# Two-attention decoder layer: an order by batch halves for the last three head groups, angles on GpSimd, and maxima turned in fp16

## The reference

```python
x = x + attn(_layernorm(x), Wq_down, Wq_up, Wq_rope, Wkv_down, Wk_up, Wv_up, Wk_rope, Wo)   # 128 heads
x = x + xattn(_layernorm(x), ctx, ctx, positions, Wq, Wk, Wv, Wo)                           # 32 heads, 8 kv heads
x = x + ffn(_layernorm(x), gate_w, base_w, base_b, lora_A, lora_B)                          # 8 LoRA experts, top 2
# attn: q_c = (x Wq_down) Wq_up, k_c and v_c from x Wkv_down: 4 wide per head; q_r = x Wq_rope: 64 per head
#       k_r = x Wk_rope, one for all heads; scores = (q_c k_c + q_r k_r) / sqrt(68); softmax; v_c; Wo
# xattn: rotary angles position * 10000^(-2i/16) turn q and k (head width 16); softmax; Wo
```

## Time and profile before

| | us |
|---|---|
| median of 3 runs | 869.03 (868.4 to 870.11) |
| the profiled execution | 867.85 |
| its span | 865.9 |
| TensorE busy | 803.9 (93%) |
| VectorE busy | 647.9 (75%) |
| ScalarE busy | 568.5 (66%) |
| GpSimd busy | 582.8 (67%) |

### The profile page before, as it was taken

How to read it: one execution, slowest core, us unless ns; L and a number is a source line. 1 busy time by engine, 2 the same in 40 slices (tenths; PEclk the granted TensorE clock), 3 DMA queues, 4 the chain that set the end, 5 groups by cost and what they waited for, 6 DMA issues and landing times.

```text
span 865.9 us, 17867 instructions
## 1 busy us (share of the span) xinstructions
PE 803.9 (93%) x5624; PEld 395.2 (46%) x5624; DVE 647.9 (75%) x1209; ACT 568.5 (66%) x1045; POOL 582.8 (67%) x492
## 2 busy tenths in 40 slices
PE   4999999999999999999999999999848688999986
PEld 3464444444454444444444444444313344555433
DVE  7866777767677888777888767788787567888754
ACT  4757777777777777777777777777530465555641
POOL 7747888888788878888888878885543223333210
PEclk9999999999999999999999999999978799999999
DMA  8344455434334332434333433432130000000001
GB/s 334 110 166 146 92 156 169 139 85 112 101 90 105 85 108 78 107 97 123 85 82 91 113 104 89 109 89 56 29 88 0 1 1 3 15 13 15 13 13 37
DMA packets 51227, 74.69 MB, mean 86 GB/s; under 512 B 9968, under 2 KB 33520, under 8 KB 50672
## 3 DMA queue, kind: packets, MB, share of 16 engines
q1 hardware_dynamic: 51184, 74.18, 30.7%
HBM read 38.16 MB, written 18.87 MB: 66 GB/s over the span
## 4 chain that ended last, share of the span: by engine, by line
PE 84%; DVE 8%; ACT 2%; issue 2%; DMA 1%; SPq 1%; POOL 0%; DVEq 0%; ACTq 0%
PE PS L1200 39%; PE PS L1152 8%; PE PS L1236 7%; PE PS L1266 6%; PE PS L1268 6%; PE PS L1283 5%; PE PS L1411 2%; PE PS L1325 1%; PE PS L1418 1%; PE PS L1380 1%; PE PS L1397 1%; PE PS L1426 1%; PE PS L1456 1%; DVE xm L1027 1%; PE PS L1244 1%
## 5 line engine op out<-in xcount | busy, mean ns | idle before, releaser
L492 POOL TENSOR_TENSOR Pl<-PR,Ph 128x512 f16<-128x512 f32 x254 | 285.8, 1157 | 24.7 <-ACT Ph L668 24.7
L661 ACT ACTIVATE PR<-PS 128x512 f32<-128x512 f32 x256 | 152.6, 597 | 135.0 <-PE PS L1268 128.5
L795 DVE TENSOR_REDUCE mneg<-PS 128x4 f32<-128x512 f32 x256 | 174.6, 684 | 38.2 <-PE PS L1236 34.7
L1200 PE MATMUL PS<-XTh,Wh 128*128 128x512 f16 x512 | 194.5, 380 | 0.0
L1200 PE MATMUL PS<-XTh,Wl 128*128 128x512 f16 x512 | 193.7, 378 | 0.0
L1200 PE MATMUL PS<-XTl,Wh 128*128 128x512 f16 x512 | 193.5, 378 | 0.0
L783 DVE SCALAR_TENSOR_TENSOR QS<-PS,QC 64x512 f16<-64x512 f32 x256 | 175.5, 686 | 18.0 <-ACT QC L593 10.9
L593 ACT ACTIVATE QC<-PS 64x512 f16<-64x512 f32 x256 | 150.7, 589 | 10.6 <-PE PS L1200 4.3
L668 ACT ACTIVATE Ph<-PR 128x512 f16<-128x512 f32 x256 | 139.3, 617 | 0.0
L474 POOL TENSOR_TENSOR Wh<-Wraw,wscale 128x1024 f16<-128x1024 f32 x32 | 60.6, 1893 | 70.8 <-PE PS L1200 67.5
L1236 PEld LDWEIGHTS PS<-KC,QC 112*128 112x128 f16 x1024 | 78.8, 97 | 62.2 <-issue 2.7
(11 more groups left out here) (213 smaller groups left out, 1163.4 us busy)
## 6 DMA issues: line engine op xcount, KB each, us to landing
Wraw<-in_wqr SPq DMA_DIRECT2D x32, 512.0 KB, 4.6
QS<-QC SPq DMA_DIRECT2D x64, 256.0 KB, 3.2
head_outputs<-OS SPq DMA_DIRECT2D x256, 40.0 KB
q_content_parts<-stg SPq DMA_DIRECT2D x12, 256.0 KB, 2.8
k_content_parts<-stg SPq DMA_DIRECT2D x12, 256.0 KB, 3.1
QC<-q_content_parts SPq DMA_DIRECT2D x128, 24.0 KB
KC<-k_content_parts SPq DMA_DIRECT2D x32, 96.0 KB
xs<-in_x SPq DMA_DIRECT2D x8, 256.0 KB, 4.5
```

The lines of the kernel that those rows point to most:

```text
L492: nc.gpsimd.tensor_tensor(Pl[:, b], PR[:, b % 4], Ph[:, b], ALU.subtract).then_inc(s_pl, 1)
L661: nc.scalar.activation(PR[:, b % 4, :], PS[:, bB[b % 2], :], ACT.Exp, scale=ATT_SCALE).then_inc(s_e, 1)
L795: nc.vector.tensor_reduce(mneg[:, par, b // 4, :, b % 4], PS[:, bA[b % 2], :].rearrange("p (j k) -> p j k", j=GH), AX.X, ALU.max, negate=T ...
L1200: last = mm(PS[:, bQ[c % 2], :], wt[:, par, k, p * P:(p + 1) * P], xt[:, k, sl], start=(k == 0 and n == 0), stop=(k == KT - 1 and n == 2))
```

## The change

1. `max_turn` and `x_max_turn` turn fp16 maxima (`mneg`, `xm`) with an fp16 identity `id16`, into an fp16 view of the bank. `id16` is made in the prologue, and the first `max_turn` waits for it.
2. `angles` runs on GpSimd in the prologue, between the memsets of V and the first `values`; a multiply and a subtract take the place of each fused operation, 24 operations in all. GpSimd also prepares a third and fourth key buffer `KC2`.
3. The halves are numbered n = 0 to 63. The last six (LATE = 58) are batches 0 to 3 of groups 29, 30, 31 and then batches 4 to 7 of groups 31, 30, 29. For these the contents come half by half, the weights of 30 and 31 are split half-wise (ScalarE the high part, GpSimd the rest), group 29's weights are stored in DRAM and read back, VectorE makes one low half of four for n = 55 and 56, and the values are copied half by half. `project` takes its eight products with Wh first.
4. T = 3 is gathered in two halves: batches 0 to 3 as soon as the even stores are out, 4 to 7 after the last. Batches 4 to 7 get their T = 0 to 2 as a partial sum, added to x at the seam (`output_part`, `x1_part`), and their last T at u = 5, 8, 11 and 15 of the cross loop, normalised at u = 1 to 4. At u = -2 TensorE waits for `s_x1` of 4.
5. The low halves of the weights wo, bw and ag of the later parts move from VectorE to GpSimd, as two operations each (`split_low`, at u = -3, 1, 2); ScalarE makes their high halves after the last weighing. Buffers are laid out anew so that this can begin while the head groups still run, and GpSimd's clearing of cross-attention buffers is partly moved forward.

The diff, cut to its core:

```diff
+def job(h):
+    if h < LATE:
+        g, t, k = h // 2, h % 2, h // 2 % 2
+    else:
+        g = G0 + h - LATE if h < TURN else NG - 1 - (h - TURN)
+        t, k = h // TURN, (0, 2, 1, 3)[h % 4]
+    return Job(g, t, h, h // 2, h // 2 % 2, h % 2, k, g % 2)
...
-        mneg = sb("mneg", [P, 2, 2, GH, B // 2])
+        mneg = sb("mneg", [P, 2, 2, GH, B // 2], F16)
...
+            def late_half(h):
+                if h == LATE:
+                    sp.wait_ge(s_ws, G0 + 1)
+                    sp.dma_start(WD[0], W16[:, G0 % 2]).then_inc(s_wst, 16)
+                    w_in(NG - 1, G0 % 2)
+                maxima(job(h - 2))
+                if h == NH - 2:
+                    sp.wait_ge(s_q, 2 * h)
+                    sp.wait_ge(s_wst, 16)
+                    sp.dma_start(W16[:, G0 % 2], WD[0]).then_inc(s_wr, 16)
+                q_again(job(h - 1))
+                if h + 1 < NH:
+                    late_contents(job(h + 1))
+                outputs(job(h - 4))
...
+            late_contents(job(LATE))
+            for h in range(LATE, NH):
+                late_half(h)
+            maxima(job(NH - 2))
+            outputs(job(NH - 4))
+            q_again(job(NH - 1))
+            maxima(job(NH - 1))
             for j in range(GH):
-                gather(KT - 1, j)
-            sp.wait_ge(s_q, 4 * NG)
+                half_quarter(0, j)
+            outputs(job(NH - 3))
+            outputs(job(NH - 2))
+            sp.wait_ge(s_b, 4 * NH)
             sp.dma_start(lb_sb[:], lb).then_inc(s_ffn, 16)
             sp.dma_start(bias[:], bb.to_broadcast([P, DM])).then_inc(s_ffn, 16)
+            outputs(job(NH - 1))
+            for j in range(GH):
+                half_quarter(1, j)
...
+            angles()
+            pool.wait_ge(s_red, 1)
+            nc.gpsimd.tensor_copy(id16, ident[:]).then_inc(s_kx, 1)
             pool.wait_ge(s_vl, B)
-            pool.wait_ge(s_zero, 4)
+            pool.wait_ge(s_kx, 1)
             values(0, 0)
...
+            def split_low(n):
+                l, w, h = ((wol, xwo_sb, woh), (bwl, bw_raw, bwh), (agl, ag_raw, agh))[n]
+                pool.wait_ge(s_xh, n + 2)
+                nc.gpsimd.tensor_tensor(w[:], w[:], wscale[:].to_broadcast(list(w.shape)), ALU.mult).then_inc(s_xw, 1)
+                pool.wait_ge(s_xw, n + 1)
+                nc.gpsimd.tensor_tensor(l[:], w[:], h[:], ALU.subtract).then_inc(s_xl, 1)
...
+            o_out(job(NH - 4))
+            q_low(job(NH - 1), 1)
+            for b in range(4):
+                row_max(job(NH - 1), b)
+            max_out(job(NH - 1))
+            normalise(KT - 2, 7)
+            x1_part(4)
+            wx_low()
+            x1_part(5)
+            o_out(job(NH - 3))
+            x1_part(6)
+            x1_part(7)
+            o_out(job(NH - 2))
+            normalise(KT - 1, 0)
+            normalise(KT - 1, 1)
             x1(0)
...
                 if u == FIRST:
+                    rope_factors()
+                if u == FIRST + 1:
+                    x1(1)
+                    k_rope(0)
+                if u == FIRST + 2:
+                    o_out(job(NH - 1))
                     normalise(KT - 1, 2)
-                    x1(1)
+                if u == FIRST + 3:
+                    x1(2)
                     normalise(KT - 1, 3)
...
+                if u == FIRST + 4:
+                    x1(3)
                 if u == FIRST + 5:
-                    for v in range(EARLY, B):
-                        x1(v)
-                    dve.wait_ge(s_x1, B)
+                    k_rope(1)
+                if 1 <= u <= 4:
+                    normalise(KT - 1, u + 3)
+                if u in LATER:
+                    x1(LATER[u])
...
-                nc.tensor.transpose(PS[0:16, bM, 0:S], mneg[:, par, t].rearrange("p j b -> p (j b)"), ident[:]).then_inc(s_mt, 1)
+            def max_turn(j):
+                if not later(j.n, 1):
+                    pe.wait_ge(s_kx, 1)
+                pe.wait_ge(s_m, 4 * j.n + 4)
+                if later(j.n, 1):
+                    pe.wait_ge(s_me, j.n)
+                nc.tensor.transpose(PM16[0:16, 0:S], mneg[:, j.p, j.s].rearrange("p j b -> p (j b)"), id16).then_inc(s_mt, 1)
...
+            for i in range(4):
+                rough_scores(job(NH - 1), i)
+                if i == 0:
+                    pe.wait_ge(s_ql, 4 * NH - 2)
+                if i < KT - 1:
+                    output_part(4, i)
+            pe.wait_ge(s_ql, 4 * NH)
+            output_part(5, 0)
+            max_turn(job(NH - 1))
+            scores(job(NH - 2), 0)
...
+            scores(job(NH - 1), 3)
+            weigh(job(NH - 2))
+            for v in range(2):
+                for T in range(KT):
+                    output(v, T)
...
                 if u == FIRST + 2:
-                    for v in range(3, EARLY):
-                        output(v, KT - 1)
+                    weigh(job(NH - 1))
+                    for T in range(KT):
+                        output(2, T)
                 if u == FIRST + 3:
-                    for v in range(EARLY, B):
-                        pe.wait_ge(s_x1, v - EARLY + 1)
-                        for T in range(KT):
-                            output(v, T)
+                    for T in range(KT):
+                        output(3, T)
+                if u in LATER:
+                    v = LATER[u]
+                    if v == B // 2:
+                        pe.wait_ge(s_oe, NH)
+                    take(bF[1], s_x1, v + 1)
+                    output(v, KT - 1)
```

More of the change, by code:

```diff
@@ L1 @@
 import math
+from collections import namedtuple
 from contextlib import ExitStack
@@ L53, with ago, later, pool_lows @@
 AG = E * R + E
+NH = 2 * NG
+QG = NG // KT
+LG = 3
+G0 = NG - LG
+LATE = NH - 2 * LG
+TURN = LATE + LG
+Job = namedtuple("Job", "g t n r p s k w")
+def job(h):
[5 more added lines that the diff above has]
+    return Job(g, t, h, h // 2, h // 2 % 2, h % 2, k, g % 2)
+def ago(g, par, t, d):
+    if isinstance(g, int):
+        return job(2 * g + t - d) if 0 <= 2 * g + t - d < NH else None
+    back = (d - t + 1) // 2
+    r, p, t = (g - back if back else g), (par + back) % 2, (t - d) % 2
+    return Job(r, t, 2 * r + t, r, p, t, p, p)
+def later(n, first):
+    return not isinstance(n, int) or n >= first
+BY_DVE = range(LATE - 3, TURN - 4)
+def pool_lows(n, b):
+    return 4 * n + b + 1 - (sum((m, 3) <= (n, b) for m in BY_DVE) if isinstance(n, int) else 0)
+def dve_lows(n):
+    return sum(m <= n for m in BY_DVE)
+def shares(h):
+    if h >= NH - 2:
+        return [(KT - 2, 4), (KT - 2, 5)] if h == NH - 2 else [(KT - 2, 6)]
+    return [(T, h - (16 * T + 26)) for T in range(KT - 1) if 0 <= h - (16 * T + 26) < B]
 def build(nc, x, ctxT, pos, wdkr, wup, wqr, wo, xwq, xwkv, xwo, bw, ag, lb, bb, out):
@@ L172, in build @@
         agl = sb("agl", [P, KT, AG], F16)
[L173 to L184, removed]
+        pn, Ah, Al = (None, pn1, pn2), (None, Ah1, Ah2), (None, Al1, Al2)
         XPT = sb("XPT", [P, 2, 2, REP * S])
@@ new lines, in w_in, with half @@
+            def w_in(g, par):
+                sp.dma_start(Wraw[:, par], wqr[bass.ds(g, 1)].rearrange("a p k n -> (a p) k n")).then_inc(s_w[par], 16)
+            def half(g, par, t):
+                J = lambda d: ago(g, par, t, d)
+                if J(2):
+                    maxima(J(2))
+                if t == 0 and reached(g, 2):
+                    contents(g, par)
+                if t == 1:
+                    sp.wait_ge(s_ws, g + 1)
+                    w_in(g + 2, par)
+                q_again(J(1))
+                if J(4):
+                    outputs(J(4))
@@ new lines, in half @@
+            def half(g, par, t):
+                J = lambda d: ago(g, par, t, d)
+                if J(1) and later(J(1).n, 2):
+                    q_high(J(1), 1)
+                if isinstance(g, int) and LATE <= 2 * g + t < TURN - 1:
+                    late_high(J(0).g + 1)
+                if J(3):
+                    p_high(J(3))
+                for b in range(4):
+                    if J(2):
+                        exps(J(2), b)
+                    if b == 0:
+                        q_high(J(0), 0)
@@ new lines, in half @@
+            def half(g, par, t):
+                J = lambda d: ago(g, par, t, d)
+                for n in range(8):
+                    project(J(0), n // KT, n % KT)
+                    if n == 0 and isinstance(g, int) and 2 * g + t == 2:
+                        pe.wait_ge(s_ul, 16)
+                        pe.wait_ge(s_vl, B)
+                        max_turn(job(0))
+                    if 1 <= n <= 4:
+                        rough_scores(J(1), n - 1)
+                    if 3 <= n <= 6:
+                        scores(J(2), n - 3)
+                    if n == 7:
+                        max_turn(J(1))
+                        if J(3):
+                            weigh(J(3))
```

795 lines of the change are left out of this document (431 added, 364 removed).

## The result

The changed kernel takes **882.1 us** (median of 4 runs, 881.85 to 883.34), against 868.7 (867.75 to 870.11) for the kernel before on the same chip: a ratio of 1.0159, 95% interval 1.0139 to 1.0178. It is slower by 1.6%, where 852.3 was forecast. The profiled execution has a span of 880.5 us against 865.9, so 14.6 us are to be found.

What follows compares the result with a forecast made beforehand. TensorE's slots were taken to set the head loop's pace, with a serial seam behind. Terms -3.0 - 1.2 + 0 + 1.6 - 22.6 + 3.5 + 2 + 3 = -16.7 gave 851.2 us profiled, 852.3 at the median; range 842 to 862.

Steps and rivals of the forecast that it cites:

- (f): Rival, prologue: GpSimd's angle operations are slow, 1.5 us each, delaying TensorE's first turn of maxima; 877 us, chance 0.05.
- a loop longer than 194 + 12 us: Sign of being wrong: the cross loop, from first turn to the end, lasts longer than that.
- Maxima in fp16: Term, turns of maxima: 0.05 us saved per turn, 3.0 us in the head loop and 1.2 in the cross loop.
- The four-pass rule: Page rule, fp32 turns: four passes would make a turn 0.21 us, the saving 0.16 each, 13 us in all.
- Angles: Term, prologue: 24 angle operations and the identity on GpSimd take 8.8 us, hidden; 0, bounds 0 and +34.
- Late halves: Term, switch to the late halves: maxima issued 3.4 us late with 1.74 slack; +1.6 us, bounds 0 and +6.
- The seam: Term, last projection (T) to first cross turn: shrinks from 64.6 to 42 us, -22.6; bounds T + 35 and T + 47.
- Handed on to the cross loop: Term, cross loop: late outputs +3.5, normalisings and additions +2, weight lows on GpSimd +3 us.
- The late outputs: Term, cross loop: four last outputs at 0.9 us each, three in the saturated part; +3.5 us.
- The lock: Term, cross loop: long GpSimd weight-low operations can each hold one VectorE operation; +3 us, range 0 to 16.
- rival (b): Cross loop: long GpSimd splits catch second k_rope, two normalisings and a rope sum, 12 us not 3; 861 us, chance 0.15.

Runs made afterwards that it cites:

- e7: e4 with the row maxima of both attentions written as fp32 again and turned by the fp32 identity: 854.6 us.
- e4: The changed kernel with the three edits of e1, e2 and e3 together: 850.3 us, ratio 0.9797 to the kernel before.
- e8: e4 with SyncE's order at the switch to the late halves made weight store, maxima, weight load: 849.5 us.
- e6: e4 with the four late outputs of token blocks 4 to 7 and their additions left out: 846.3 us.
- e1: The changed kernel with GpSimd's first weight low, split_low(0), waiting until VectorE's second k_rope is through: 874.8 us.
- e2: The changed kernel with VectorE's additions of the late outputs put ahead of the same turn's row maxima instead of last: 862.8 us.
- e5: e4 with the two other weight lows made on GpSimd in turns 5 and 6 instead of 1 and 2: 848.4 us.
- e3: The changed kernel with SyncE issuing the maxima ahead of the weight store and next weights' load at the switch to the late halves: 876.7 us.

## Why the prediction was wrong

The forecast of the sign and the size failed on two of its terms; the others came out or nearly so. 882.1 lies outside every rival too; the only slower one, (f), named another place. One of the signs of being wrong did come: a loop longer than 194 + 12 us.

- **Maxima in fp16.** Head turns: 0.07 a half instead of 0.05. T came 3.6 later with 7.05 lost at the switch, so they brought some 3.4 us instead of 3.0. Cross turns: 0.04 each, some 1.0 us, where 1.2 was forecast. Together 4 to 5 measured (e7: 4.3 over e4, 5.1 over e8), 4.2 forecast. The row behind the forecast was an odd one, though: only 2 of the old kernel's 64 head turns have the next matmul 0.11 us behind them, as in the earlier trace rows; 62 have it after 0.20 or 0.21. In the cross loop the distance from a turn of maxima to the next product is mostly 0.20 or 0.21 in fp32 and 0.15 or 0.16 in fp16. Transposes of one shape in a row start 0.11 apart in fp32 (the four of L1734 in e4, at 771.43) and 0.06 in fp16. So 0.09 us stand behind a cross turn in either type, and they drop out of the difference: the forecast's 0.05 is right there, its slots are not. The four-pass rule of the Trainium skill (FP8 and Floating Point Precision, TensorE Precision Notes), by which an estimate of the saving was 13 us, isn't borne out for these transposes: 0.11 in a row is half of the 0.21 worked out from it, and changing the turns back costs 0.07 and 0.04 each.
- **Angles**: 0 forecast, and 0 in the trace, where GpSimd still waits 0.98 us for V behind them; rival (f) is false. Its operations took 0.43 each, not 1.5.
- **Late halves**: the step that failed in part. The forecast priced the queue by issue times (3.4 late, 1.74 slack, +1.6). The late contents cost 1.68 to issue and not 3.30, and the maxima went out 1.5 us late by their turn and not 3.4. By issue times alone there was no stall to come. But 1 MB stood ahead of their 4 KB, and they landed 6.3 us later and not 1.8. Measured: the distance of turns 15.78 instead of 8.73, +7.05, outside the term's bounds of 0 to +6 (14.3 to 16.2 from turn to turn in the three profiled executions with this order). The place was named, the mechanism wasn't.
- **The seam**: T + 41.6 against T + 42. The steps came out as well: the outputs of batch 0 start at T + 17.7 (18.0 forecast), those of batch 1 end at T + 25.3 (25.2), and the first cross projection starts at T + 31.4 (31). The term that carried the forecast is right, and by its mechanism.
- **Handed on to the cross loop**: the step that failed. It was 3.5 + 2 + 3 = 8.5 (7.3 with the cross turns) and came to 34.0. The late outputs cost 3 to 5 (e6). The lock was foreseen as a mechanism, and its place, the second k_rope, stood in rival (b); the 12 us of that rival were too much and the 3 of the sum too little: 3 to 5.5 (e1, e4 against e2), and 1.4 to 1.9 for the other places (e5). What no term and no rival had is the bank: 18.1 us between the first and the last turn, 19.3 at the medians (e2). The forecast counted the four additions as VectorE time, 0.7 us each, and never asked where in VectorE's round they stand, and who waits for the bank that they free. With that order repaired, and with the lock's and the switch's, the loop is 202.8 us in e4 and 201.0 in e8: 8.7 and 6.9 over the old one, where 7.3 was the sum.

So e4, at 850.3, is close to the kernel that the forecast described, 852.3. In part that is luck: against the old kernel's its stages are -2.4, -23.9 and +8.7, where -1.4, -22.6 and +7.3 were forecast, and the misses offset each other. The forecast priced the work that was moved and took the handshakes around it as free.

In all, as far as the runs separate it: seam -23.0; switch +7; fp16 turns -3.4 ahead of T. Of the +32.6 between the first and the last cross turn 18.1 are the bank (e2), 5.5 the lock (e4 against e2), and 5.0 the late outputs (e6 against e4). 4.0 are left for four normalisings, the lock's other places and the low clock of the loop's start, less the fp16 turns. That remainder wasn't tried by itself, and each of these figures is uncertain by the 2 us of a single execution.

## What to carry to other kernels

When an operation is moved into a loop that rotates buffers, price its place in the consumer's queue, not only its length: four additions of 0.7 us cost 18 to 19 us here, because each stood last in its round and the bank that it frees was the next one wanted. Put the read that frees a shared bank as early as its operand is there. Likewise, a small transfer that an engine is waiting for goes ahead of the large ones of its queue; and a long GpSimd operation goes beside VectorE work that has slack, or behind it.

## What the runs showed of the hardware

- A 4 KB transfer issued right behind a 512 KB store and a 512 KB load on the same queue landed after 6.3 us. Behind the store alone it landed after 3.5 (e8), ahead of both after 1.8 (e3), the median of all.
- Some of VectorE's fp32 operations between SBUF tiles, started beside a GpSimd one of 128x2048, ended only with it or up to 0.7 us behind it: 4.08 us instead of 0.68, 2.44 for pn instead of 0.55, 3.17 for a 128x128 product instead of 0.29. A reciprocal of 128x128 kept its 0.94. The Trainium skill (SBUF — State Buffer, SBUF: two separate sides) calls the shared port an exclusive lock, and the rows of the held operations agree. What a lock costs the kernel hangs on the slack of the operation that it holds: 3.2 to 5.5 of the 6.8 us won by the third turn were left at the end, and 1.4 to 1.9 of 4.3 us in the later places.
- GpSimd's single operations on 128x64 fp32 took 0.24 to 0.43 us, about 0.1 less than the distance from one to the next.
- The stalls went with more than their length: with 12.2 us of waits at the bank gone, the turns took 18.1 us less. TensorE's granted clock stood at 0.83 to 0.91 over the stretch with them, and at 1.00 from 720 on without.
- One transpose has no single price. In fp32 the next matmul started 0.11 us behind it in a row of equal transposes, and 0.20 to 0.21 behind nearly every turn of maxima, ahead of `weigh` or `x_scores`. In fp16 it was 0.06 in a row and 0.15 to 0.16 ahead of `x_scores`. The difference of the two types, 0.05, was the same in both places.
